# The second expert loop's switch, its gathers and the turns of layer 4, moved

## The reference

```python
x = x + _L0_xattn_ref(_layernorm(x), ctx, ...)   # layer 0: attention, 8 heads, windows
x = x + _L0_ffn_ref(_layernorm(x), ...)          # layer 1: 8 experts, the best one for each row
x = x + _L1_xattn_ref(_layernorm(x), ...)        # layer 2: attention, 16 heads
x = x + _L1_ffn_ref(_layernorm(x), ...)          # layer 3: 16 experts, the best three for each row
x = x + _L2_xattn_ref(_layernorm(x), ...)        # layer 4: attention, 16 heads, causal mask
x = x + _L2_ffn_ref(_layernorm(x), ...)          # layer 5: ternary weights, squared relu
x = x + _L3_xattn_ref(_layernorm(x), ...)        # layer 6: attention, key mask
x = x + _L3_ffn_ref(_layernorm(x), ...)          # layer 7: tables picked for each row, splines
```

```python
raw_gate = softmax(x @ gate); _, topk_idx = top_k(raw_gate, 3)
gate_topk = mask * raw_gate / sum(abs(mask * raw_gate))
hidden = relu(einsum('btd,edh->bteh', x, W1) + b1)
expert_out = einsum('bteh,ehd->bted', hidden, W2) + b2
return einsum('bte,bted->btd', gate_topk, expert_out)
```

## Time and profile before

| | us |
|---|---|
| median of 3 runs | 524.5 (523.93 to 524.78) |
| the profiled execution | 521.5 |
| its span, first to last instruction | 519.8 |
| TensorE busy | 407.3 (78%) |
| TensorE's weight loads busy | 338.1 (65%) |
| VectorE busy | 336.0 (65%) |
| ScalarE busy | 238.7 (46%) |
| GpSimd busy | 229.0 (44%) |

### The profile page before, as it was taken

One profiled execution on the slowest core, in us unless ns is written; L12 is line 12 of the kernel. 1 busy time (PEld: TensorE's weight loads), 2 busy tenths in 40 slices (PEclk: granted clock), 3 DMA queues, 4 the chain that ended last, 5 costly groups with the idle time before them and its releaser, 6 DMA issues.

```text
span 519.8 us, 9990 instructions
## 1 busy us (share of the span) xinstructions
PE 407.3 (78%) x2628; PEld 338.1 (65%) x2628; DVE 336.0 (65%) x1142; ACT 238.7 (46%) x635; POOL 229.0 (44%) x290
## 2 busy tenths in 40 slices
PE   5787748999788989879899945984999999953350
PEld 4676738899466778569799843763866778743340
DVE  5846534656578765625445646867757688678887
ACT  2332304566354532357677624343755475642230
POOL 2611770014631767754357777464112355351224
PEclk9796557999999975779999979696999999985555
DMA  7799764796165111134436522110000000000002
GB/s 203 238 393 408 220 177 133 256 307 225 52 215 206 45 47 42 46 111 123 120 119 163 144 61 57 26 36 0 1 2 1 0 1 1 1 1 1 0 1 81
DMA packets 60548, 55.42 MB, mean 107 GB/s; under 512 B 11922, under 2 KB 46446, under 8 KB 60366
## 3 DMA queue, kind: packets, MB, share of 16 engines
q1 hardware_dynamic: 53214, 43.64, 25.9%
q0 software_dynamic: 4736, 9.71, 6.4%
q10 hardware_dynamic: 2544, 1.44, 0.9%
HBM read 24.10 MB, written 30.67 MB: 105 GB/s over the span
## 4 chain that ended last, share of the span: by engine, by line
PE 29%; DVE 18%; SPq 13%; DMA 13%; POOL 8%; issue 8%; DVEq 5%; ACT 4%; POOLq 0%; ACTq 0%
SPq L436 13%; DMA outbuf<-h_sb,slots 7%; PE bank L2256 6%; PE bank L2269 6%; PE bank L2110 4%; PE bank L2126 3%; PE bank L2115 2%; PE bank L2248 2%; POOL vZ L674 2%; ACT xn L1637 2%; POOL rstd L628 2%; DMA h_sb<-outbuf,slots 2%; DVE stats L831 2%; DMA vZ<-outbuf,slots 1%; PE bank L2399 1%
## 5 line engine op out<-in xcount | busy, mean ns | idle before, releaser
L628 POOL TENSOR_TENSOR rstd<-veps,mhalf 128x4 f32<-128x4 f32 x32 | 33.8, 1056 | 111.7 <-DVE veps L836 111.4
L1731 ACT ACTIVATE r<-bank,b 128x128 f32<-128x128 f32 x218 | 65.8, 365 | 35.3 <-PE bank L2256 33.9
L2269 PE MATMUL bank<-wall,r 128*128 x436 | 67.5, 287 | 7.8 <-DVE h_sb L1304 6.7
L674 POOL DMA_INDIRECT vZ<-outbuf,slots x40 | 39.5, 987 | 56.3 <-DMA outbuf<-h_sb 42.1
L2269 PEld LDWEIGHTS bank<-wall,r 128*128 128x128 f32 x436 | 57.3, 197 | 10.4 <-issue 8.7
L647 POOL DMA_INDIRECT outbuf<-h_sb,slots x48 | 46.9, 977 | 28.2 <-DMA outbuf<-h_sb,slots 15.9
L2256 PE MATMUL bank<-on,e_sb 128*128 128x128 f32 x348 | 57.2, 296 | 0.0
L2126 PE MATMUL bank<-vB,eT 128*128 128x36 f32 x384 | 50.9, 282 | 0.0
L2126 PEld LDWEIGHTS bank<-vB,eT 128*128 128x128 f32 x384 | 50.8, 207 | 0.0
L1310 DVE COPY e_sb<-wall 128x256 f32 (+1 forms) x75 | 24.7, 333 | 40.3 <-PE bank L2256 25.1
L2256 PEld LDWEIGHTS bank<-on,e_sb 128*128 128x128 f32 x348 | 48.1, 204 | 0.7 <-issue 0.2
(11 more groups left out here) (305 smaller groups left out, 854.3 us busy)
## 6 DMA issues: line engine op xcount, KB each, us to landing
outbuf<-zero SPq DMA_DIRECT2D x17, 1024.0 KB, 12.7
wall<-in_w SPq DMA_DIRECT2D x4, 2048.0 KB, 13.7
outbuf<-h_sb SPq DMA_DIRECT2D x66, 64.0 KB
h_sb<-outbuf SPq DMA_DIRECT2D x63, 64.0 KB, 1.9
h_sb<-rowbuf SPq DMA_DIRECT2D x23, 64.0 KB, 2.7
outbuf<-h_sb POOLq DMA_DIRECT2D x20, 64.0 KB, 2.0
x<-in_x ACTq DMA_DIRECT2D x4, 256.0 KB, 6.4
b2all<-in_L_ffn_b SPq DMA_DIRECT2D x1, 1024.0 KB, 15.5
```

Source lines behind the costliest of these rows:

```text
L628: r = nc.gpsimd.tensor_tensor(rstd[:, at], veps[:, at], mhalf[:, 0:W], ALU.pow)
L674: nc.gpsimd.indirect_dma_start(tile_of(yg[l][b], w * K + k), None, outbuf[0:MOE[l][0] * REGION * P], bass.IndirectOffsetOnAxis(slots[:, c: ...
L1731: i = a.activation(hT[:, u * 512 + c * P:u * 512 + (c + 1) * P], bank[2 + u][:, c * P:(c + 1) * P], ACT.Relu, bias=b1[l][:, bass.ds(e * C ...
L2269: y = mm(bank[6 + s % 2][:, 0:P], hT[:, (s % 2) * 512 + c * P:(s % 2) * 512 + (c + 1) * P], wall[:, bass.ds(e * n + (WHALF + c * P), P)], ...
```

## The change

Four things are moved. (1) The first EARLY[3] slots are 12 instead of 16, and with them the slots at which the second list is made and read (LISTED, TURNED, FROM). (2) Batch 0's gathers are bound to slot 26 instead of 30, and GpSimd stores slots 8 to 27 instead of 12 to 31. (3) On GpSimd all gathers of batch 3 stand ahead of `power(18)`, the power of batch 2, and `power(16)` and `power(17)` one and four gathers later. (4) In layer 4 batches 1, 2 and 3 are normalised and turned at tiles 1, 5 and 9 instead of 0, 4 and 8. The arithmetic is the same; lines behind L727 stand two lines higher.

```diff
--- before.py
+++ after.py
@@ -45,19 +45,19 @@
 SLOT_TILES = {l: T * TOPK[l] + MOE[l][0] - 1 for l in MOE}
 PLACES = 8
 KINDS = 4
-PRIOR = {1: (11, 15, 19, 23), 3: (31, 39, 51, 63)}
-SHARE = range(12, 32)
+PRIOR = {1: (11, 15, 19, 23), 3: (27, 39, 51, 63)}
+SHARE = range(8, 28)
 UNDER_WAY = {1: 2, 3: 3}
-EARLY = {1: 4, 3: 16}
+EARLY = {1: 4, 3: 12}
 AHEAD = 31
-FROM = {1: 3, 3: 8}
+FROM = {1: 3, 3: 6}
 WHOLE = 3
-LISTED = {1: (1, 2), 3: (3, 6)}
-TURNED = {1: 0, 3: 4}
+LISTED = {1: (1, 2), 3: (2, 4)}
+TURNED = {1: 0, 3: 3}
 LAG = 4
 ROUND = 1.5 * 2.0 ** 30
 RING = 4
-LATE = (0, 4, 8)
+LATE = (1, 5, 9)
 REGION = T + 1
 GRID = 16
 TAB = 4 * GRID + 1 + D
@@ -724,14 +724,12 @@
                 tile_stores(s, s + 10)
             gather(3, 0)
             gather(3, 1)
-            gather(3, 2, 0, 3)
+            gather(3, 2, 0, 4)
             power(16)
-            gather(3, 2, 3, 8)
+            gather(3, 2, 4)
             power(17)
-            gather(3, 2, 8)
-            gather(3, 3, 0, 5)
+            gather(3, 3)
             power(18)
-            gather(3, 3, 5)
             add_bo(0)
             add_bo(1)
             power(19)
```

## The result

The changed kernel took 529.45 us (median of 20 runs), the kernel before 524.69 in as many: 1.0084 times the time before, 95% interval 1.0062 to 1.0107, so 4.4 us slower (3.3 to 5.6). One run of the changed kernel fell in a slower state and is left out of the ratio; the two medians as they stand are 4.8 apart. The forecast was 3.1 us slower, 527.6 us. The profiled execution took 527.13 us, its span is 525.4 and its mean granted clock 0.836.

What follows compares the result with a forecast made beforehand. Bounds named: VectorE's 6.0 us wait for gathered rows behind GpSimd's chain, and layer 4's waits for normalised rows. A 2.5 us gain and 5.6 us loss gave +3.1, 527.6 us, range 522.6 to 531.4.

Steps and rivals of the forecast that it cites:

- the three waits at batch 3: Layer 4, before tile 12: norm behind tile 10's exponential, layer 5's norm behind power 20, turn copy behind both; loss 4.4 to 5.3 us.
- The stop at slot 12: Second expert loop: slot 12's load waits for the last scatter, its turn 3.7 us late, then two slow slots.
- Batch 0's gathers: GpSimd, bound to slot 26: they start at 269.1, 0.9 us earlier, where four slots would have been 4.7.
- The attention starts 2.2 earlier: After the expert loop: 0.9 us from earlier gathers plus 1.3 from the last slots running at 2.4 GHz.
- GpSimd becomes the bound of batch 2's power: With batch 3's gathers ahead of it, batch 2's power starts at 334.9 without idle time; batch 2 is not earlier.
- Batch 3's rows no longer waited for, 2.3 us: VectorE in layer 4's attention: the wait of 1.50 us goes, and the adds gain 0.77 more.
- The gain by tile 10, 2.5 us: Layer 4's attention: tile 10 at 355.0, from a range of 353.4 to 355.6, a gain of 2.5 us so far.
- The backlog at 1.2 GHz, up to 1.5: After tile 12's scores TensorE works off its backlog at 1.2 GHz; VectorE's next step waits up to 1.5 us more.
- Rival 1: Faster: the expert loop is not held at slot 12, batch 0's gathers start 4.8 us earlier; 522.6 us, chance 0.11.
- rival 4: The waits of the three turns in layer 4's attention vanish as a whole, some -11 us: 513, chance 0.02.
- Rival 3: Slower: loads of slots 13 to 16 late too, GpSimd gains nothing, loss 7 us; +6.0, 530.5 us, chance 0.21.
- Rival 2: Same: TensorE keeps 2.4 GHz in the attention, gain 4.1 and loss 4.4 us; +0.3, 524.8 us, chance 0.10.

Runs made afterwards that it cites:

- e11: Kernel before with only layer 4's turns moved to tiles 1, 5 and 9: 530.15 us, 1.0118 of before (1.0044 to 1.0192).
- e4: Changed kernel with power 20 ahead of batch 3's bias add on GpSimd, on a slower chip: 585.2 us, 1.0157 of before (1.0079 to 1.0236).
- e8: Changed kernel with power 20 ahead of batch 3's bias add and layer 5's norm behind batch 3's turn copy: 527.6 us, 1.0038 of before.
- e7: Kernel before with 12 first tiles alone, batch 0's gathers still bound to slot 30: 530.85 us, 1.0133 of before (1.0066 to 1.02).
- e9: Kernel before with the two expert loop edits alone, 12 first tiles and batch 0 bound to slot 26: 523.3 us, 0.9978 of before.
- e10: Changed kernel with layer 4's turns back at tiles 0, 4 and 8, on a faster chip: 526.9 us, 1.002 of before (0.998 to 1.0061).
- e6: Changed kernel, unchanged, run again beside the kernel before on one chip: 531.6 us, 1.0104 of before (1.0058 to 1.015).
- e5: Kernel before, unchanged, profiled again on a chip like the first: 526.1 us.
- e2: Changed kernel with layer 4's turns back at tiles 0, 4 and 8, on a slower chip: 580.8 us, 1.0089 of before (1.004 to 1.0139).
- e12: Kernel before with the two expert loop edits plus 64 identity transposes on TensorE ahead of batch 3's turn, slower chip: 568.2 us, 0.9974 of before.
- e3: Changed kernel with batch 3's turn alone back at tile 8, on a slower chip: 581.9 us, 1.0146 of before (1.007 to 1.0221).

## Why the prediction was right, point by point

The direction and the main term came from the mechanism: the three waits at batch 3 were forecast at 4.4 to 5.3 us, measured 4.9, and e11, e4 and e8 show them one by one. The sum came within 1.3 us, but its other half, the gain ahead of tile 10, was put too high, so the 3.1 forecast lies a little under what the runs leave open (3.3 to 5.6).

Times of the changed profile are taken 0.9 us less here, for its later slot 0.

- **The stop at slot 12** (load at 241.09, turn at 243.1, clock low behind it): measured 240.9 and 242.7. Right, and e7 shows it alone. The two slow slots were 1.97 and 1.66 us instead of 2.14 each, so slot 27 turned at 261.7 and not 262.8. (The stall that the prediction puts down to the earlier trace rows is the one of the earlier trace rows.)
- **Batch 0's gathers** (269.1, within 267 to 270): 268.0. The binding gains 4.7 and more, the hold gives most of it back (3.9 in e7): 1.4 to 2.0 stay in the changed kernel, e8, e9 and e10, 1.0 in e6.
- **VectorE's wait at slot 59** (1.3): 1.38. Right.
- **The attention starts 2.2 earlier**: 1.7 in the first pair, 0.3 in the second. Over all fast chips slot 0 to tile 0 took 92.2, 91.3 and 90.9 us with the old loop (before, e5, e11) and 90.5, 91.1, 92.2, 90.7 and 90.0 with the new one (after, e6, e8, e9, e10): 0.6 less on the mean, which is less than either group spreads. This term was too large. Of the 1.3 us that I gave to the last slots at 2.4 GHz the traces show 0.4: from VectorE's step at slot 59 to tile 0 it is 13.2 before and 12.8 after. The clock did fall in the changed kernel too (0.50 from about 304.1 to 307.5, before from 303.4 to 310.3). But that is not what was missing: in e9 it stood at 1.00 from 303 to 316, and the stretch still took 12.8.
- **GpSimd becomes the bound of batch 2's power** (334.9, no idle time): 335.2, none. Right, and in e10 against e9 it costs 2.4 us of wait at tile 7. Tile 8 was put at 340.9 to 341.8 and came at 342.5: GpSimd was 0.3 later, and TensorE made batch 2's turn as well as its scores at 1.2 GHz (0.50 from 338.2 to 345.0), where I had taken that level for the scores alone.
- **Batch 3's rows no longer waited for, 2.3 us**: right, 1.50 and 0.77. The gathers were no slower beside VectorE, as I took it: the last two, at 333.91 and 335.16 in its trace, took 0.95 and 0.94 us.
- **The gain by tile 10, 2.5 us**: 1.4 in the first pair, a loss of 0.8 in the second (e5, e6). The step that failed in size is this one, through the start of the attention and tile 8.
- **Three waits at batch 3** (tile 12 10.3 to 11.3 us behind tile 10, VectorE idle 6 to 7): 10.9 and 7.32. e4 took the second wait away and gained 1.6 at tile 12, e8 the second and third and gained 3.2; e11 has all of them without the rest of the change.
- **The backlog at 1.2 GHz, up to 1.5**: 1.0. The loss from tile 10 on was 6.0 where I took 5.6. (My upper bound of 7.3 for it does not follow from its terms, 5.3 + 1.5 = 6.8.)
- **Sum**: -2.5 + 5.6 = +3.1 was forecast; the first pair of profiles has -1.4 + 6.0 + 0.1 = +4.7, the runs say +4.4; the second pair has +0.8 + 6.0 = +6.8, the runs beside it +5.5.

Rival 1 (slot 12 not held) fell to the turns of slots 11 and 12, rival 4 to the wait of 7.32 us. Rival 3 (6 us, with no gain for GpSimd) describes e6 in part: nearly no gain ahead of tile 10, though GpSimd's gathers did start 1.0 sooner. Rival 2 had the clock at 2.4 GHz in the attention; it fell to 1.2 three times there, around the turns of batches 1, 2 and 3. I had no rival in which the price of the old order is itself not fixed. In the kernel before the new turns cost 6.0 us (e11). But with the moved gathers the old turns already have a tail of 17.3 us (e10, and e2), so there the new turns cost only 3.4, and the rest comes with the gathers' move (17.3 in e10 against 14.9 in e9, on one chip). I had credited that move with 2.3 us and charged it nothing in the tail; that my loss of 5.6 came out right for all four edits together is in this respect luck.

The Trainium skill ("TensorE: Matmul & The Clock Gate", Part 1) has TensorE's low clock as the default that activity releases. The trace agrees: e12, with activity where the others idle, kept 1.00 from 382 to 412.

Left open: what the later turns of batches 1 and 2 cost by themselves (e11's tile 0 to tile 10 is 41.5, 0.9 more than before, but holds both and the clock), and what stalls the loop on the slower chips.

## What to carry to other kernels

Before a step is moved one place later, read what then stands directly ahead of it and behind it on its engine: here a copy fell behind a norm of the next layer, and that norm hung on a second engine's queue. A switch moved earlier gains only up to the event that it waits for, here the last scatter. And TensorE idling ahead of a burst on the critical path pays for the idle time again in the burst: 13.9 us for the tail without the idle time, 14.7 to 17.4 with it. So when an edit takes a wait away, read the granted clock behind it too before the gain is booked: here 2.3 us gained at one wait went with 2.5 lost a few tiles on.

## What the runs showed of the hardware

TensorE's granted clock came back to 1.00 3 to 4 us after it took up the turn of batch 3 (before, e5, e9) or more than 8 (e7, e10, e2, e3), with the same instructions from tile 10 on. In all seven profiles it had stood at 0.50 for 10.2 us; what differed was whether it fell 6.5 to 6.9 or 1.3 to 1.7 us ahead of the turn. This goes with 2.5 us in the tail, which is more than the loop's whole gain. With 64 transposes in the idle time it did not fall (e12).

The same kernel took 525 to 526 us on three chips and 568.6 and 578.2 on two others, where VectorE stands 7 to 10 us several times in the expert loop; the cause is open.
